# A vision tower with a mixture of experts: the high and the low half of the second FFN matrix side by side, in one 512-column product

## The chip, the cores and the metric

The kernel runs on one core of a Trainium2 chip, as one program with one launch. The metric is the device time in microseconds (us). The kernel before takes 1067.86 us, the median of three runs (1067.56 to 1068.58).

## The reference, cut to what matters

Sixteen images of 256 tokens with 256 features pass through a token mixer (16 independent sequences), a gated linear recurrence, and then an FFN with one shared and eight routed experts. Only the FFN bears on the change:

```python
def new_gelu(x):
    c = math.sqrt(2.0 / math.pi)
    return 0.5 * x * (1.0 + jnp.tanh(c * (x + 0.044715 * x * x * x)))

def _moe_forward(x, Wfc_s, bfc_s, Wproj_s, bproj_s, Wr, Wfc, bfc, Wproj, bproj):
    xf = x.reshape(Bb * Tt, C)                       # C = 256, hidden 1024
    shared = new_gelu(xf @ Wfc_s + bfc_s) @ Wproj_s + bproj_s
    ...                                              # softmax over 8 experts, top 2, gates sum to 1
    for e in range(N_EXPERTS):
        h = new_gelu(xf @ Wfc[e] + bfc[e]) @ Wproj[e] + bproj[e]
        routed = routed + h * gate[:, e:e + 1]
    return (shared + routed).reshape(Bb, Tt, C)
```

The class token's row is the same for all images before the FFN, and the kernel computes it once.

## The kernel before, in words

**Precision.** The big products run in fp32r, a format that the matrix engine takes in one pass but rounds. To keep accuracy each operand is split into a high half (rounded) and a low half (the rest), and a product is the sum of three: high x high, high x low and low x high. For the second FFN product the operands are G, the hidden activations (`GH`, `GL`, 1024 hidden rows in 8 parts of 128, by 256 tokens), and the second matrix (`W2H`, `W2L`, 8 parts of 128 rows by 256 columns). G is the stationary operand (128 x 128, loaded as weights), the matrix is the moving one.

**First stage, the mixer (`steps`).** A software pipeline over the images: step t projects image t, and at the same time computes later phases of images t-1 to t-4. The last phase is the shared expert for image t-4: for j in 0 to 7 the first product `fc` (6 products), and, three parts later (`LAG = 3`), the second one, `project_hidden` for part j-3. VectorE (`DVE`) computes `GL` for each part (`low_g`, L1077), waits for it on `y_ps` at the end, adds the bias into `yb` (L1425) and the residual (L1428). The accumulators `y_loop` share the two PSUM banks of `ps_nd` with the mixer's numerator and denominator (L843), of which they take the first half.

**Second stage, the experts (`experts_tensor`, `experts_vector`, `experts_pool`).** Tokens were scattered into lists by expert. Eight experts follow each other, each with its blocks of 256 tokens (36 in all here, read from register bounds). The matrix engine (`PE`) does per block: `fc` for the parts 0 to 7, the hidden parts 0 to 4 between them, the transposes of the next block's rows (L892), and the hidden parts 5 to 7. At the first hidden part it waits until `y_done` says that VectorE has read the accumulators. VectorE does per block: `GL` for eight parts, the low half of the next tokens (`xl`, L1485), then `rows_to` (L1543), which waits until the row adds of the block before have landed (`added`), a copy of `info` (L1480), two adds of the bias to `yt` (L1548), one for each half of the tokens, and two products with the gate to `yb` (L1552). Then the next block's `GL`. In the last block of an expert it also subtracts the low halves of the next expert's weights between the `GL` operations (`low_w`, L1518); at its end it counts `expert_done`.

GpSimd (`POOL`) waits for `y_done` of each block, starts two indirect DMAs that add the 256 rows to the output (L603), and, when an expert starts, before its blocks: `load_high` and `load_stage`, four DMAs of 1 MB for the next expert, each on the same DMA queue as the row adds. Its small `carrier` operations mark where it waited: `carrier_pool` for `added`, `carrier_y` for `y_done`.

**Semaphores.** `gh_done`, `gl_done`: a part of GH or GL is there. `y_ps`: the sum of one half of the tokens is complete. `y_done`, `yt_done`: VectorE's operations at L1425 / L1552, and at L1548. `w_split`: the low halves of an expert are there.

## Time and profile before

| | |
|---|---|
| median of three runs | 1067.86 us |
| the profiled execution, its own time | 1067.47 us |
| its span, first to last instruction | 1065.7 us |
| mean granted TensorE clock | 0.955 |
| PE busy | 91% |
| DVE busy | 66% |
| ACT busy | 43% |
| POOL busy | 35% |

The span has a beginning (about 120 us) in which the pipeline fills, the mixer in its regular steps of 32 us to about 600 us, and the experts from there to the end. Busy time of PE counts the modelled ends of its products, which overlap; what a product takes from the engine is seen from the distance of two starts in the timeline. In a timeline "x2" means that two instructions of one kind were merged to one row.

### The profile page before, as it was taken

Reading aid. Unit: us, or ns where it says so; the run is one execution under the profiler, and the core shown is the slowest. Engines: PE = TensorE matmul, PEld = TensorE weight load, DVE = VectorE, ACT = ScalarE, POOL = GpSimd, SP = SyncE. Lnnn points to the kernel's source line nnn. Section 1 sums busy time; section 2 is a strip of 40 time slices with the busy share of each in tenths; the row PEclk is TensorE's granted clock in tenths of the full one; section 3 lists DMA queues with packets and bytes.
Section 4 is the critical chain, followed back from the end, with each engine's and each line's share of the span. In section 5 each row is a group of like instructions: output and inputs, shape, how many; then the busy total and the mean of one; then the engine's idle time right before and its main releaser. Section 6 shows DMA issues by size and latency. Waiting matters only on the chain.

```text
span 1065.7 us, 21605 instructions
## 1 busy us (share of the span) xinstructions
PE 970.7 (91%) x6889; PEld 899.1 (84%) x6890; DVE 705.3 (66%) x2095; ACT 454.7 (43%) x1139; POOL 378.0 (35%) x468
## 2 busy tenths in 40 slices
PE   5787788999999999999788999999999999999995
PEld 3555587888888888888787899999999999999995
DVE  3458788887887877888776446464645546564643
ACT  2011143344444444444332255555555555555553
POOL 4232554242343243343421133443243424243222
PEclk9667799999999999999999799999999999999998
DMA  9300610111100111100011372837272633664322
GB/s 275 104 10 11 173 40 1 40 42 40 40 20 22 38 40 40 40 20 15 32 45 41 122 202 45 208 52 190 40 212 45 168 79 80 163 129 126 45 40 31
DMA packets 48164, 82.68 MB, mean 78 GB/s; under 512 B 6416, under 2 KB 30883, under 8 KB 48132
## 3 DMA queue, kind: packets, MB, share of 16 engines
q0 software_dynamic: 31056, 57.46, 22.3%
q1 hardware_dynamic: 17076, 24.84, 7.9%
q8 instruction: 15, 0.25, 0.1%
q14 instruction: 17, 0.14, 0.0%
HBM read 55.32 MB, written 26.96 MB: 77 GB/s over the span
## 4 chain that ended last, share of the span: by engine, by line
PE 41%; issue 27%; DVE 15%; POOL 13%; ACT 1%; POOLq 1%; DMA 0%; DVEq 0%; SPq 0%; ACTq 0%
PE ps_nd L657 14%; PE ps_proj L642 8%; POOL out L603 5%; PE ps_proj L722 5%; PE ps_ri L642 4%; DVE rden L1254 3%; PE ps_ip L642 3%; POOL v_rows L498 2%; PE ps_nd L843 2%; POOL h L561 1%; PE ps_h L830 1%; PE ps_h L815 1%; POOL rstd L494 1%; PE ps_t L729 1%; DVE A L1386 1%
## 5 line engine op out<-in xcount | busy, mean ns | idle before, releaser
L1077 DVE TENSOR_TENSOR GL<-g_act,GH 128x256 fp32r<-128x256 f32 (+1 forms) x424 | 185.3, 439 | 189.4 <-ACT GH L955 170.3
L657 PE MATMUL ps_nd<-w2h,GH 128*128 128x256 f32 x832 | 248.9, 299 | 24.9 <-DVE GL L1077 13.5
L950 ACT ACTIVATE g_act<-ps_proj,fcb 128x256 f32<-128x256 f32 (+1 forms) x280 | 130.8, 468 | 308.8 <-PE ps_proj L642 300.6
L657 PE MATMUL ps_nd<-w2l,GH 128*128 128x256 f32 x832 | 235.8, 283 | 0.0
L657 PE MATMUL ps_nd<-w2h,GL 128*128 128x256 f32 x832 | 234.7, 282 | 0.0
L657 PEld LDWEIGHTS ps_nd<-w2h,GH 128*128 128x128 f32 x832 | 158.4, 190 | 35.2 <-DVE GL L1077 14.0
L955 ACT CAST GH<-g_act 128x256 fp32r<-128x256 f32 x416 | 161.4, 397 | 0.0
L657 PEld LDWEIGHTS ps_nd<-w2l,GH 128*128 128x128 f32 x832 | 158.8, 191 | 0.0
L657 PEld LDWEIGHTS ps_nd<-w2h,GL 128*128 128x128 f32 x832 | 158.1, 190 | 0.0
L642 PE MATMUL ps_proj<-xh,w1h 128*128 128x256 f32 x544 | 116.3, 295 | 9.3 <-issue 4.4
L603 POOL DMA_INDIRECT out<-yb,rows_to x72 | 114.8, 1595 | 16.7 <-issue 12.8
L642 PE MATMUL ps_proj<-xl,w1h 128*128 128x256 f32 x544 | 110.3, 285 | 0.0
L642 PE MATMUL ps_proj<-xh,w1l 128*128 128x256 f32 x544 | 108.7, 281 | 0.0
L491 POOL TENSOR_TENSOR ve<-mv,eps 128x2 f32<-128x2 f32 x48 | 10.4, 218 | 276.6 <-DVE mv L1092 276.6
L642 PEld LDWEIGHTS ps_proj<-xh,w1h 128*128 128x128 f32 x544 | 85.3, 190 | 16.7 <-issue 10.8
L722 PE MATMUL ps_proj<-wproj,x 65*128 65x256 f32 x256 | 78.9, 459 | 12.8 <-DMA x<-x 6.4
L642 PEld LDWEIGHTS ps_proj<-xl,w1h 128*128 128x128 f32 x544 | 84.2, 190 | 0.0
L642 PEld LDWEIGHTS ps_proj<-xh,w1l 128*128 128x128 f32 x544 | 83.7, 189 | 0.0
L722 PEld LDWEIGHTS ps_proj<-wproj,x 65*128 65x128 f32 x256 | 66.8, 327 | 19.5 <-issue 15.0
L498 POOL DMA_INDIRECT v_rows<-v,slots x64 | 68.2, 1065 | 35.9 <-DVE slots L1362 19.1
L331 POOL TENSOR_TENSOR carrier_y<-minus_half 1x1 f32<-1x1 f32 x36 | 6.6, 183 | 175.3 <-DVE yb L1552 175.3
L961 ACT ACTIVATE E<-ps_proj 128x256 f32<-128x256 f32 x32 | 12.3, 383 | 118.2 <-PE ps_proj L722 118.1
(271 smaller groups left out, 1943.4 us busy)
## 6 DMA issues: line engine op xcount, KB each, us to landing
R<-v_rows SPq DMA_DIRECT2D x37, 260.0 KB
w1h<-fc_w POOLq DMA_DIRECT2D x9, 1024.0 KB
w2h<-pj_w POOLq DMA_DIRECT2D x9, 1024.0 KB
stage<-fc_w POOLq DMA_DIRECT2D x9, 1024.0 KB
stage<-pj_w POOLq DMA_DIRECT2D x9, 1024.0 KB
v_rows<-tail_rows SPq DMA_DIRECT2D x16, 260.0 KB, 3.0
x<-x SPq DMA_DIRECT2D x16, 256.0 KB, 3.6
out<-yb SPq DMA_DIRECT2D x16, 256.0 KB, 2.1
```

The source lines that it names most:

```text
L494: pool.tensor_tensor(rstd[i][:], ve[i][:], minus_half[:], ALU.pow).then_inc(rstd_done[i], 1)
L498: pool.indirect_dma_start(out=v_rows, out_offset=bass.IndirectOffsetOnAxis(ap=where_to, axis=0), in_=source, in_offset=None).then_inc(sema ...
L603: pool.indirect_dma_start(out=out, out_offset=bass.IndirectOffsetOnAxis(ap=rows_to[:, a:a + 1], axis=0), in_=yb[:, a, :], in_offset=None, ...
L642: last = pe.matmul(dst, w[a][:, k, cols], rhs, start=(q == 0), stop=(q == len(parts) - 1))
L657: last = pe.matmul(banks[a], g[:, j, a * P:(a + 1) * P], w[i][:, j, :], start=(j == 0 and q == 0), stop=(j == HT - 1 and q == 2))
L722: last = pe.matmul(ps_proj[:, h, :], head_view(par, lt, h), wproj[:, h, :], start=True, stop=True)
L843: last = pe.matmul(ps_nd[:, tt, :], ewT[:, s, tt * P:(tt + 1) * P], E[:, s, :], start=(s == 0), stop=(s == LT - 1))
L950: act.activation(g_act[:, j % G_SLOTS, 0:width], banks[j % len(banks)][:, 0:width], ACT.Gelu_apprx_tanh, bias=fcb[i][:, j:j + 1]).then_inc ...
L955: act.copy(GH[:, j, :], g_act[:, j % G_SLOTS, :]).then_inc(gh_done, 1)
L961: act.activation(E[:, lt, M:2 * M].rearrange("p (h d) -> p h d", h=H), ps_proj[:, :, D:2 * D], ACT.Exp).then_inc(exp_done, 1)
L1077: dve.tensor_tensor(GL[:, j, 0:width], g_act[:, j % G_SLOTS, 0:width], GH[:, j, 0:width].bitcast(F32), ALU.subtract).then_inc(gl_done, 1)
L1254: dve.reciprocal(rden[:, tt, :], ps_nd[:, tt, M:2 * M]).then_inc(recip_done, 1)
```

## The change

`W2H` and `W2L` become one buffer `W2` with 512 columns per part: the high half in columns 0 to 255, the low half in 256 to 511. The accumulators become 512 columns wide, a whole PSUM bank. Per hidden part and half of the tokens there are now two products: GH with all 512 columns (its left half is high x high, its right half high x low), and GL with the left 256 columns, added onto the left half. VectorE adds the left half and the bias, and then the right half, in two more operations per block or image. PE's wait at the first hidden part of an expert's block is now on `yt_done`.

```diff
-        W2H = [sb(f"w2h{i}", [P, HT, M], F32R) for i in range(2)]
-        W2L = [sb(f"w2l{i}", [P, HT, M], F32R) for i in range(2)]
+        W2 = [sb(f"w2_{i}", [P, HT, 2 * M], F32R) for i in range(2)]
...
-        y_loop = [ps_nd[:, 0, 0:M], ps_nd[:, 1, 0:M]]
+        y_loop = [ps_nd[:, 0, :], ps_nd[:, 1, :]]
...
-            pool.dma_start(W2H[i][:], pj_of(g)).then_inc(high_loaded, 16)
+            pool.dma_start(W2[i][:, :, 0:M], pj_of(g)).then_inc(high_loaded, 16)
...
+        def low_part(eng, i, q, parts):
+
+            half = parts // 2
+            if q < half:
+                n = FT * HID // half
+                cols = slice(q * n, (q + 1) * n)
+                return eng.tensor_tensor(flat(W1L[i])[:, cols], flat(stage1)[:, cols],
+                                         flat(W1H[i])[:, cols].bitcast(F32), ALU.subtract)
+            n = HT // half
+            js = slice((q - half) * n, (q - half + 1) * n)
+            return eng.tensor_tensor(W2[i][:, js, M:2 * M], stage2[:, js, :],
+                                     W2[i][:, js, 0:M].bitcast(F32), ALU.subtract)
...
             for a in range(2):
-                for q, (g, w) in enumerate(((GH, W2H), (GH, W2L), (GL, W2H))):
-                    last = pe.matmul(banks[a], g[:, j, a * P:(a + 1) * P], w[i][:, j, :],
-                                     start=(j == 0 and q == 0), stop=(j == HT - 1 and q == 2))
+                tokens = slice(a * P, (a + 1) * P)
+                pe.matmul(banks[a], GH[:, j, tokens], W2[i][:, j, :], start=(j == 0), stop=False)
+                last = pe.matmul(banks[a][:, 0:M], GL[:, j, tokens], W2[i][:, j, 0:M], start=False,
+                                 stop=(j == HT - 1))
...
                         if j == LAG:
-                            pe.wait_ge(y_done, b * 2 + 2 * SBLK)
+                            pe.wait_ge(yt_done, b * 2 + 2)
...
-                        dve.tensor_tensor(yb[:, a, :], y_loop[a], pjb[0][:], ALU.add
+                        dve.tensor_tensor(yb[:, a, :], y_loop[a][:, 0:M], pjb[0][:], ALU.add
+                                          ).then_inc(y_half, 1)
+                    for a in range(2):
+                        dve.wait_ge(y_half, 2 * n + a + 1)
+                        dve.tensor_tensor(yb[:, a, :], yb[:, a, :], y_loop[a][:, M:2 * M], ALU.add
                                           ).then_inc(y_done, 1)
...
-                    dve.tensor_tensor(yt[:, a, :], y_loop[a], pjb[i][:], ALU.add
+                    dve.tensor_tensor(yt[:, a, :], y_loop[a][:, 0:M], pjb[i][:], ALU.add
+                                      ).then_inc(yt_half, 1)
+                for a in range(2):
+                    dve.wait_ge(yt_half, b * 2 + (a + 1))
+                    dve.tensor_tensor(yt[:, a, :], yt[:, a, :], y_loop[a][:, M:2 * M], ALU.add
                                       ).then_inc(yt_done, 1)
-                dve.wait_ge(yt_done, b * 2 + 2)
+                dve.wait_ge(yt_done, b * 2 + 4)
```

The class token's products (L922) are changed in the same way: 24 become 16, and its three additions on VectorE stay three.

PE in an expert's block, from `fc` of one part over a hidden part to the next `fc`. Before (`w2h1` and `w2l1` are the high and the low half in the second of two buffers):

```order
L642 MATMUL ps_proj<-xl0,w1h1 128x256 x2
L654 REGISTER_ALU
L657 MATMUL ps_nd<-w2h1,GH 128x256
L657 MATMUL ps_nd<-w2l1,GH 128x256
L657 MATMUL ps_nd<-w2h1,GL 128x256
L657 MATMUL ps_nd<-w2h1,GH 128x256
L657 MATMUL ps_nd<-w2l1,GH 128x256
L657 MATMUL ps_nd<-w2h1,GL 128x256
L642 MATMUL ps_ri<-xh0,w1h1 128x256 x2
```

The same place in the changed kernel, where `w2_1` is the second of the two joint buffers:

```order
L651 MATMUL ps_proj<-xl0,w1h1 128x256 x2
L663 REGISTER_ALU
L666 MATMUL ps_nd<-w2_1,GH 128x512
L667 MATMUL ps_nd<-w2_1,GL 128x256
L666 MATMUL ps_nd<-w2_1,GH 128x512
L667 MATMUL ps_nd<-w2_1,GL 128x256
L651 MATMUL ps_ri<-xh0,w1h1 128x256 x2
```

Nothing changes its place against `fc`; six products have become four.

VectorE at the end of an expert's block, from the wait for the row adds to the next block's first GL. Before:

```order
L1543 CAST rows_to<-info 128x2 [waits added]
L1480 COPY info<-R 128x8 [waits rows_loaded]
...
L1548 TENSOR_TENSOR yt<-ps_nd,pjb1 128x256 [waits y_ps]
L1547 REGISTER_ALU
L1548 TENSOR_TENSOR yt<-ps_nd,pjb1 128x256 [waits y_ps]
L1550 REGISTER_ALU
L1552 TENSOR_SCALAR yb<-yt,gate 128x256 [waits yt_done]
L1552 TENSOR_SCALAR yb<-yt,gate 128x256
```

In the changed kernel:

```order
L1554 CAST rows_to<-info 128x2 [waits added]
L1495 COPY info<-R 128x8 [waits rows_loaded]
...
L1559 TENSOR_TENSOR yt<-ps_nd,pjb1 128x256 [waits y_ps]
L1558 REGISTER_ALU
L1559 TENSOR_TENSOR yt<-ps_nd,pjb1 128x256 [waits y_ps]
L1562 REGISTER_ALU
L1563 TENSOR_TENSOR yt<-yt,ps_nd 128x256 [waits yt_half]
L1562 REGISTER_ALU
L1563 TENSOR_TENSOR yt<-yt,ps_nd 128x256 [waits yt_half]
L1565 REGISTER_ALU
L1567 TENSOR_SCALAR yb<-yt,gate 128x256 [waits yt_done]
L1567 TENSOR_SCALAR yb<-yt,gate 128x256
```

The two gate products, and with them `y_done` and the next block's `GL`, now stand behind four adds instead of two.

## Rows read from the trace of the kernel before

**Rows 1.** The page, part 1: busy us, share of span, instructions.

```profile
PE 970.7 (91%) x6889; PEld 899.1 (84%) x6890; DVE 705.3 (66%) x2095; ACT 454.7 (43%) x1139; POOL 378.0 (35%) x468
```

**Rows 2.** Windows: stretch, us; busy PE PEld DVE ACT POOL; PEclk, DMA share, GB/s.

```profile
300.00:400.00 100.00, 94.44 (x626) 84.57 (x625) 83.29 (x251) 43.94 (x103) 36.00 (x44) 1.00 0.09 32
...
800.00:900.00 100.00, 97.50 (x812) 96.30 (x811) 57.51 (x172) 53.42 (x138) 34.99 (x43) 1.00 0.42 87
```

**Rows 3.** PE timeline, one block (start, us, instruction); last row: groups, 600 to 1066.

```profile
843.74 0.60 PE L892 MATMUL ps_t<-ident,R 128*128 128x128 f32 x4
...
850.74 0.28 PE L657 MATMUL ps_nd<-w2h,GH 128*128 128x256 f32 x1
...
851.45 0.40 PE L642 MATMUL ps_proj<-xh,w1h 128*128 128x256 f32 x2
...
855.71 0.60 PE L892 MATMUL ps_t<-ident,R 128*128 128x128 f32 x4
...
L657 PE MATMUL ps_nd<-w2l,GH 128*128 128x256 f32 x576 | 162.2, 282 | 0.0
```

**Rows 4.** Timeline of PE and its weight loads (PEld) in the mixer.

```profile
384.70 0.37 PE L804 MATMUL ps_ri<-route_hl,xh 128*128 128x16 f32 x2
384.92 0.37 PE L804 MATMUL ps_ri<-route_hl,xl 128*128 128x16 f32 x2
...
389.55 1.97 PE L830 MATMUL ps_h<-outw_sb,YT 128*128 128x256 f32 x8
391.36 1.02 PE L843 MATMUL ps_nd<-E,ewT 128*128 128x512 f32 x2
...
391.79 0.19 PEld L843 LDWEIGHTS ps_nd<-E,ewT 128*128 128x128 f32 x1 [0.24 <-issue]
392.22 0.19 PEld L843 LDWEIGHTS ps_nd<-E,ewT 128*128 128x128 f32 x1 [0.24 <-issue]
```

**Rows 5.** DVE timeline, end of a common block; in brackets idle before, releaser.

```profile
845.60 0.16 DVE L1543 CAST rows_to<-info 128x2 uint32<-128x2 f32 x1
...
846.15 0.78 DVE L1548 TENSOR_TENSOR yt<-ps_nd,pjb 128x256 f32<-128x256 f32 x2
846.97 0.62 DVE L1552 TENSOR_SCALAR yb<-yt,gate 128x256 f32<-128x256 f32 x2
848.73 0.42 DVE L1077 TENSOR_TENSOR GL<-g_act,GH 128x256 fp32r<-128x256 f32 x1 [1.14 <-issue]
```

**Rows 6.** Timelines of DVE and PE at two hand-overs to the next expert.

```profile
772.59 0.50 PE L642 MATMUL ps_proj<-xh,w1h 128*128 128x256 f32 x2 [1.01 <-DVE xl L1485]
...
775.11 0.43 DVE L1077 TENSOR_TENSOR GL<-g_act,GH 128x256 fp32r<-128x256 f32 x1 [0.47 <-issue]
...
831.29 0.42 DVE L1077 TENSOR_TENSOR GL<-g_act,GH 128x256 fp32r<-128x256 f32 x1
...
831.83 0.32 PE L657 MATMUL ps_nd<-w2h,GH 128*128 128x256 f32 x1
...
834.24 0.50 PE L642 MATMUL ps_proj<-xh,w1h 128*128 128x256 f32 x2 [1.50 <-issue]
...
836.75 0.43 DVE L1077 TENSOR_TENSOR GL<-g_act,GH 128x256 fp32r<-128x256 f32 x1 [0.66 <-ACT GH L955]
```

**Rows 7.** Timelines of POOL and DVE: late row adds, second block of two experts.

```profile
795.17 0.18 POOL L331 TENSOR_TENSOR carrier_pool<-minus_half 1x1 f32<-1x1 f32 x1 [5.20 <-DMA out<-yb,rows_to]
...
858.10 0.18 POOL L331 TENSOR_TENSOR carrier_pool<-minus_half 1x1 f32<-1x1 f32 x1 [6.50 <-DMA out<-yb,rows_to]
...
858.05 0.17 DVE L1543 CAST rows_to<-info 128x2 uint32<-128x2 f32 x1 [0.40 <-DMA out<-yb,rows_to]
```

**Rows 8.** Timelines of PE and DVE, end of a mixer step.

```profile
381.53 0.39 PE L657 MATMUL ps_nd<-w2h,GH 128*128 128x256 f32 x1 [0.64 <-issue]
...
383.01 0.69 DVE L1428 TENSOR_TENSOR yb<-yb,h 128x512 f32<-128x512 f32 x1
385.50 0.42 DVE L1247 TENSOR_TENSOR E<-ps_proj,E 128x256 f32<-128x256 f32 x1 [1.80 <-ACT xr L967]
```

More of the change, by code:

```diff
@@ L274, in vit_tower @@
         y_ps, y_done, yt_done, sum_done = sem("y_ps"), sem("y_done"), sem("yt_done"), sem("sum_done")
+        y_half, yt_half = sem("y_half"), sem("yt_half")
         info_done, added = sem("info_done"), sem("added")
@@ L480, in split_low @@
             for q in range(PARTS) if part is None else (part,):
-                stage, high, low = ((stage1, W1H, W1L), (stage2, W2H, W2L))[q * 2 // PARTS]
-                n = 2 * FT * HID // PARTS
-                cols = slice((q % (PARTS // 2)) * n, (q % (PARTS // 2) + 1) * n)
-                last = pool.tensor_tensor(flat(low[i])[:, cols], flat(stage)[:, cols],
-                                          flat(high[i])[:, cols].bitcast(F32), ALU.subtract)
+                last = low_part(pool, i, q, PARTS)
             if part in (None, PARTS - 1):
@@ L920, in experts_tensor @@
             for j in range(HT):
-                for q, (g, w) in enumerate(((GH, W2H), (GH, W2L), (GL, W2H))):
-                    last = pe.matmul(y_loop[0][0:2, :], g[:, j, 0:2], w[0][:, j, :],
-                                     start=(j == 0 and q == 0), stop=(j == HT - 1 and q == 2))
+                pe.matmul(y_loop[0][0:2, :], GH[:, j, 0:2], W2[0][:, j, :], start=(j == 0),
+                          stop=False)
+                last = pe.matmul(y_loop[0][0:2, 0:M], GL[:, j, 0:2], W2[0][:, j, 0:M], start=False,
+                                 stop=(j == HT - 1))
             last.then_inc(y_ps, 2)
@@ L1496, in experts_vector @@
             dve.wait_ge(y_ps, 2 * b + 2)
-            for a in range(2):
-                cols = slice(a * P, (a + 1) * P)
-                dve.tensor_tensor(c_y[:, cols], y_loop[0][0:1, cols], pjb[0][0:1, cols], ALU.add
-                                  ).then_inc(y_done, 1)
+            dve.tensor_tensor(c_y[:], y_loop[0][0:1, 0:M], pjb[0][0:1, :], ALU.add
+                              ).then_inc(y_done, 2)
             dve.wait_ge(y_done, 2 * b + 2)
+            dve.tensor_tensor(c_y[:], c_y[:], y_loop[0][0:1, M:2 * M], ALU.add).then_inc(yt_done, 2)
+            dve.wait_ge(yt_done, 2)
             dve.tensor_tensor(c_y[:], c_y[:], c_h1[:], ALU.add).then_inc(cls_base, 1)
@@ L1510, in low_w @@
             def low_w(g, i, j):
-                stage, high, low = ((stage1, W1H, W1L), (stage2, W2H, W2L))[j * 2 // HT]
-                n = 2 * FT * HID // HT
-                cols = slice((j % (HT // 2)) * n, (j % (HT // 2) + 1) * n)
                 if j == 0:
@@ L1517, in low_w @@
                     dve_wait(dve, high_loaded, g * 32 + 32, "wh")
-                last = dve.tensor_tensor(flat(low[i])[:, cols], flat(stage)[:, cols],
-                                         flat(high[i])[:, cols].bitcast(F32), ALU.subtract)
+                last = low_part(dve, i, j, HT)
                 if j == HT - 1:
```

## The prediction

> **What bounds the kernel now.** I read the busy shares first, then the stretches, then the order of instructions on the matrix engine (PE) inside one block. PE is busy 91% of the span [rows 1]; in the stretch of the experts it is 97% busy while VectorE (DVE) is at 58%, and in the stretch of the mixer PE has 94% and DVE 83% [rows 2]. So the experts hang on PE, whose clock is granted in full there (1.00, which is 2.4 GHz). A block of 256 tokens takes 11.97 us from one set of row transposes to the next [rows 3]. This repeats, except at the seven places where one expert hands over to the next; there PE idles another 1.01 us (772.59) or 1.50 us (834.24) [rows 6]. Inside a block the products stand without gaps: six of the second FFN matrix take from 850.74 to 851.45, 0.118 us each [rows 3]. The durations of 0.28 us overlap; only the distance of two starts is a price. The product count is 576 of each of the three kinds in the expert stretch, 16 per block, so 36 blocks [rows 3], and 256 of each in the mixer (16 images). The 0.118 us is not the price of 256 columns alone. Where a product has only 16 columns, two starts are still 0.111 us apart (0.22 for two) [rows 4]: that is the weight load. A product with 256 columns is then nearly in balance between load and stream, and pays a little over both.
>
> **The change on PE.** Per hidden part and half of the tokens it removes three products of 256 columns (3 x 0.118 = 0.355 us) and adds one of 512 and one of 256. The columns streamed are the same, 768; a weight load goes. The trace has no 512-column product of this format (fp32r), so I bound it. 
>
> On this the Trainium skill has a rule, in "TensorE: Matmul & The Clock Gate", section "Back-to-back issue gap": a warm product takes its columns over 2.4 GHz plus about 2.5 ns, which would be 216 and 109 ns, and a saving of 29 ns per pair. The same section gives 131 ns as a sustained distance at 512 columns; the trace speaks against that, since even 256 columns take 118 ns here [rows 3].
>
> **What the saving meets in the experts.** Four terms go back.
> (1) In the last block of an expert DVE also splits the next weights, and PE's last hidden part waits for GL: the product at 831.83 is stretched to 0.32 behind the GL operation at 831.29 [rows 6]. Work after the seventh hidden product hangs on DVE there, and so half of the block's 0.33 is not seen: 7 x 0.165 = 1.2 us.
> (2) DVE gets two more adds per block. Two such adds stand at 0.78 us [rows 5], so they add 0.78. In a common block DVE is idle before the first GL of the next block for 1.14 us [rows 5]: hidden, 0.36 to spare. Behind the adds in DVE's queue stand the two gate products, then this GL, for which PE's first hidden product waits. Where an expert ends, the idle time before that GL is only 0.66 us in one kind of loop turn and 0.47 in the other [rows 6], so GL comes 0.12 or 0.31 later. PE waits for exactly that. At 0.25 each, 7 x 0.25 = 1.7 us.
> (3) The later adds also delay y_done, and behind it in POOL's queue stand the row adds to the output and then the loads of the next weights. The row adds of an expert's first block queue behind these 4 MB of loads and land late: at 795.17 and 858.10, with PE's restart at 772.59 and 834.24, that is 22.58 and 23.86 us after the restart, the earliest and the latest of six [rows 6, 7]. DVE wants them for rows_to in the second block: at 858.05 it had waited 0.40, so it wants them 23.41 us after the restart. After the change the shorter blocks make it want them 0.33 + 0.20 earlier and the late GL 0.25 later, at 23.13; they land 0.78 later, at 23.36 to 24.64. DVE is late by 0.2 to 1.5 us. The cover: from rows_to to the first GL there are 3.13 us now [rows 5], 3.0 after the change, of which DVE needs 2.0 (rows_to to the end of yb) plus 0.78. So 0.25 is free, a bit more where y is already there. The wait on PE is 0 to 1.25 us, and I take 0.5: 6 x 0.5 = 3.0 us.
> (4) After the last block the adds stand before the last row adds and the copy of the class rows, which end the kernel: 0.8 us.
> PE's new wait on yt_done in place of y_done costs nothing: these adds stand ahead of GL in DVE's queue, and PE waits for GL in the same place.
>
> **The mixer.** A step there is a ring: PE, then DVE, then PE. PE stands 0.64 us before the last hidden product, which waits for DVE's last GL [rows 8], so only about four of the eight hidden parts lie on the path: 8 x 0.0205 = 0.16 us per step, 12 steps, 1.9 us; the four steps that drain have more of PE in them, 0.2 each: 0.8. The two new adds stand behind the last hidden product: yb's last add ends at 383.70 and DVE then idles 1.80 us until PE and ScalarE bring the next image [rows 8]; 0.78 fits in. Sum 2.7 us. If that cover were gone it would cost 16 x 0.78 = 12 us.
>
> The weights' split writes the same number of elements in two runs of 256 instead of one of 512, the load writes the same 1 KB rows: nothing for either. The class token's 24 narrow products become 16 and its adds stay three: under 0.5 us, left out.
>
> **Sum.** 11.9 + 2.7 - 1.2 - 1.7 - 3.0 - 0.8 = 7.9 us off. The profiled execution took 1067.47 us, 0.4 below the median shown (1067.86); its span is 1065.7. From the median: 1060.0.
>
> **The rivals.**
> (A) Forecast: 1060.0, between 1057 and 1062.5 as the stalls of (2) and (3) fall. Chance 0.50.
> (B) The short product's extra belongs to each product: 512 columns cost 0.226 (0.215 plus the same 0.011). The saving is 0.011 per pair: 6.3 + 1.5 = 7.8, less 0.6, 1.7, 2.4 (blocks shorten less, so rows are wanted later) and 0.8, 2.3 off: 1065.5. For it: the fp32 passes of 256 pay 0.011 too. Against: those of 512 do not. Chance 0.19.
> (C) The whole gain. Either the 256-column product behind a long one falls to 0.111 (the load's floor), pair 0.326, 0.028 saved: 16.1 in the experts and 3.7 in the mixer, less 1.6, 1.7, 4.2 (the stalls grow as the blocks shorten) and 0.8, which is 11.5 off; or the loads do not move with y_done and the stalls of (3) stay near nothing: 14.6 - 1.2 - 0.8 - 0.5: 12.1 off. Either way about 1056. Against it: POOL's queue is strictly behind y_done at the hand-over. The Trainium skill's rule above (109 ns behind a long product) would end here. Chance 0.20.
> (D) Slower. A 512-column product costs as much as the two it replaces, 0.236, because what bounds the stream is the moving rows, not the load. Then PE gains nothing, terms (2) and (4) stay with 1.7 and 0.8, and (3) with 1.0 (rows are wanted at 23.66, only the latest are late): 3.5 on, 1071.4. For it: at 256 columns load and stream cannot be told apart in this trace. Against it: the fp32 stream of 512 shows 0.43 per pass, not 0.452. It decides from about 0.230 us per long product; below that the saving, some 0.65 us for each nanosecond per pair, outweighs the terms. Chance 0.08.
> The rest, 0.03, is for what I have not seen.
>
> **The numbers.** A measurement of this kernel tells about 0.2% from no change, 2.1 us. Faster by more than that: A, C, and a little more than half of B: 0.84. Within: the rest of B and what of D comes out small, 0.08. Slower: 0.08. The range reaches over C and most of B: 1054.5 to 1066.
>
> **What would show it.** On PE the start behind a long product should come 0.216 us after it, behind a short one 0.118; a common block should be 11.64 us long instead of 11.97. At an expert's first GL, DVE's idle time should be gone. In six experts' second block rows_to should wait for the row adds by 0.2 to 1.5 us, and PE's first hidden product of the third block should come late. The mixer's step should shrink by 0.1 to 0.2 us of 32. I am wrong if a block keeps 11.97, if the block shrinks and the second blocks show no waits, or if DVE's adds come to stand in the mixer's ring.

## The result, and the profile after

The changed kernel takes 1071.22 us (median of 8 runs, 1069.7 to 1073.42), the kernel before 1067.86 in the same comparison (1067.09 to 1069.16). The ratio is 1.003, 95% interval 1.0019 to 1.0041: 3.4 us slower, where 7.9 us off were predicted. The number lies beside rival (D), 1071.4, but its mechanism does not hold, as will be seen. Two further timings of the changed kernel gave 1.0017 and 1.0047.

The first row of the page answers to [rows 1]:

```profile
PE 966.2 (90%) x6049; PEld 853.6 (80%) x6050; DVE 739.8 (69%) x2199; ACT 455.2 (43%) x1139; POOL 375.9 (35%) x468
```

The loads of PE fell from 6890 to 6050 as planned, but its busy time by 4.5 us only, and DVE has 34.5 us more. The two stretches of [rows 2]:

```profile
300.00:400.00 100.00, 94.79 (x573) 81.73 (x572) 85.41 (x257) 42.60 (x100) 35.29 (x45) 1.00 0.09 32
800.00:900.00 100.00, 97.22 (x681) 89.81 (x681) 63.18 (x189) 53.07 (x136) 33.40 (x41) 1.00 0.41 86
```

PE is as full as before in both, and still at 1.00 of its clock. PE in the experts, against [rows 3]: the start of the last five pairs of a block's second product, the product that follows them, and the starts of two consecutive blocks:

```profile
848.67 0.39 PE L666 MATMUL ps_nd<-w,GH 128*128 128x512 f32 x1
848.89 0.28 PE L667 MATMUL ps_nd<-w,GL 128*128 128x256 f32 x1
849.01 0.39 PE L666 MATMUL ps_nd<-w,GH 128*128 128x512 f32 x1
...
850.29 0.28 PE L667 MATMUL ps_nd<-w,GL 128*128 128x256 f32 x1
850.41 0.40 PE L651 MATMUL ps_proj<-xh,w1h 128*128 128x256 f32 x2
...
884.09 0.38 PE L902 MATMUL ps_t<-ident,R 128*128 128x128 f32 x2
...
895.95 0.38 PE L902 MATMUL ps_t<-ident,R 128*128 128x128 f32 x2
```

Five pairs take 850.41 - 848.67 = 1.74 us, 0.348 each: the long product is followed after 0.22 to 0.24, the short one after 0.12. A block takes 11.87 us (the median over all common blocks; the two starts above give 11.86) where it took 11.97 [rows 3].

To see where the time goes I cut each trace at two marks: the class rows' first transposes, which end the mixer, and, in the mixer, VectorE's first addition into E for the last image (15). From that mark on no new image enters; it lies in step 15, and what follows up to the class rows I call the drain. (The regular steps of 32 us thus end at about 510 us, not at 600 as said above.) Between images 5 and 15 every kernel here takes 322.3 to 323.1 us: **the live steps gained nothing and lost nothing that shows**. Half clock is the sum of the stretches at granted clock 0.50 that lie in the drain; a stretch of 10.2 us that begins 5 to 7 us before the drain's end and runs past it is in every trace, and its part ahead of the mark is counted. All times are us, from one trace each; the ratios are from the timed runs.

| kernel | mixer | its drain | half clock in it | experts to the end | ratio to before (95%) |
|---|---|---|---|---|---|
| before | 607.21 | 126.03 | 13.7 | 458.45 | |
| before, again | 607.18 | 123.86 | 5.2 | 458.88 | 0.9995 (0.9983-1.0007) |
| changed | 611.70 | 128.30 | 9.5 | 457.85 | 1.003 (1.0019-1.0041) |
| again | 612.14 | 129.91 | 17.4 | 458.27 | 1.0017 (1.0002-1.0033) |
| again2 | 615.87 | 132.43 | 23.6 | 457.83 | 1.0047 (1.003-1.0064) |
| experts_three | 611.77 | 129.86 | 17.6 | 458.55 | 1.0036 (1.0024-1.0049) |
| drain_only | 612.79 | 128.95 | 16.8 | 458.53 | 1.0048 (1.0035-1.0061) |
| mixer_three | 610.29 | 129.44 | 20.4 | 457.40 | 1.0008 (0.999-1.0026) |
| drain_three | 606.59 | 122.52 | 6.9 | 458.04 | 1.0018 (1.0006-1.003) |
| drain_three2 | 609.70 | 125.71 | 13.5 | 457.73 | 1.0019 (1.0008-1.0029) |
| no_adds | 610.56 | 126.86 | 11.7 | 456.13 | 0.9963 (0.9947-0.9979) |
| adds_only | 614.21 | 130.26 | 11.6 | 461.16 | 1.0075 (1.0052-1.0099) |
| act_half | 610.38 | 127.05 | 11.8 | 460.03 | 1.0008 (0.9995-1.002) |
| pool_bias | 606.91 | 124.95 | 12.6 | 460.64 | 1.0019 (1.001-1.0028) |
| pool_early | 606.04 | 124.94 | 12.6 | 455.77 | 0.9969 (0.9959-0.9979) |

So in the traces of the changed kernel the mixer ends 4.5 to 8.7 us later, and the experts take 0.2 to 1.1 us less. Not all of the mixer's difference is the drain's. The mark of image 15 falls between 480.85 and 484.07 us in the fifteen traces (before 481.18 and 483.32; changed 483.40, 482.23 and 483.44), and that goes with the place of the first half-clock stretch: the earlier it starts (26.7 to 29.7 us), the earlier image 5 has its mark (157.9 to 161.7), in one and the same order in kernels with the change and without. The change has no part in that. That both mixers of before end at 607.2 is therefore chance: the second one entered its drain 2.1 us later and had one 2.2 us shorter. The drains of the changed kernel are 2.3 to 8.6 us longer than those of before, at different amounts of half clock.

### The profile page after: what moved, and what is told of

Same layout as the page of the kernel before. It is cut to its first block, busy times and chain, and to the rows that moved or that the text cites. A ratio compares the mean times of both kernels' runs of the same rounds, so it can differ in the third digit from the quotient of the medians.

```text
span 1069.5 us, 20103 instructions
## 1 busy us (share of the span) xinstructions
PE 966.2 (90%) x6049; PEld 853.6 (80%) x6050; DVE 739.8 (69%) x2199; ACT 455.2 (43%) x1139; POOL 375.9 (35%) x468
## 4 chain that ended last, share of the span: by engine, by line
PE 41%; issue 27%; DVE 15%; POOL 12%; ACT 1%; POOLq 1%; DMA 0%; DVEq 0%; another core or an unknown queue 0%; SPq 0%; ACTq 0%
PE ps_nd L666 9%; PE ps_proj L651 8%; POOL out L612 5%; PE ps_proj L732 5%; PE ps_nd L667 4%; PE ps_ri L651 4%; DVE rden L1265 3%; PE ps_ip L651 2%; PE ps_nd L853 2%; POOL v_rows L507 2%; PE ps_h L840 2%; POOL h L570 1%; PE ps_h L825 1%; PE ps_t L739 1%; POOL rstd L503 1%
## 5 line engine op out<-in xcount | busy, mean ns | idle before, releaser
L666 PE MATMUL ps_nd<-w,GH 128*128 128x512 f32 x832 | 319.3, 410 | 27.5 <-DVE GL L1088 15.1
L667 PE MATMUL ps_nd<-w,GL 128*128 128x256 f32 x832 | 234.4, 282 | 0.0
L666 PEld LDWEIGHTS ps_nd<-w,GH 128*128 128x128 f32 x832 | 157.3, 189 | 64.3 <-DVE GL L1088 19.3
L667 PEld LDWEIGHTS ps_nd<-w,GL 128*128 128x128 f32 x832 | 157.4, 189 | 0.0
L732 PEld LDWEIGHTS ps_proj<-wproj,x 65*128 65x128 f32 x256 | 66.9, 328 | 19.6 <-issue 14.8
L853 PE MATMUL ps_nd<-E,ewT 128*128 128x512 f32 x128 | 60.2, 615 | 1.6 <-DVE E L1258 1.6
L1265 DVE RECIPROCAL rden<-ps_nd 128x256 f32<-128x256 f32 x32 | 55.7, 1740 | 4.3 <-PE ps_nd L853 4.3
```

The source lines that it names most:

```text
L666: pe.matmul(banks[a], GH[:, j, tokens], W2[i][:, j, :], start=(j == 0), stop=False)
L667: last = pe.matmul(banks[a][:, 0:M], GL[:, j, tokens], W2[i][:, j, 0:M], start=False, stop=(j == HT - 1))
L732: last = pe.matmul(ps_proj[:, h, :], head_view(par, lt, h), wproj[:, h, :], start=True, stop=True)
L853: last = pe.matmul(ps_nd[:, tt, :], ewT[:, s, tt * P:(tt + 1) * P], E[:, s, :], start=(s == 0), stop=(s == LT - 1))
L1265: dve.reciprocal(rden[:, tt, :], ps_nd[:, tt, M:2 * M]).then_inc(recip_done, 1)
```

## The experiments

**The same kernels again.** `again`, `again2`: the changed kernel without an edit; `before2`: the kernel before.

> The changed kernel once more, for a second profile of it. Theory 1 (the adds on VectorE cost the mixer its time): the time is again about 1071.2 us, and the class rows' transposes that end the mixer start again 3 to 4.5 us later than in the kernel before (607.2 us). Theory 2 (the loss in the mixer is the place at which PE's half-clock stretches happened to fall in one profile): the mixer's end lies anywhere from 607 to 612, and the median is still some 1071 only if something in the experts is worse than the profile showed.

> The changed kernel once more, on the chip of the next three: 3 to 4 us above the kernel before, as in its first two timings (ratios 1.003 and 1.0017). Both theories expect the same; it is the measure for them.

> The kernel before once more, for a second profile. If the half-clock stretches fall where they like, the class rows' transposes start at another time than 607.2 us, by more than 1 us; if the mixer is steady, at 607.2 within 0.5.

Measured: 1072.07, 1071.32 and 1067.72 us. The slowdown is there in all three timings of the changed kernel, between 1.8 and 5 us by the ratios. The launches of one kernel lie 2 to 8 us apart in one timing (1067.80 to 1075.57 in `again2`); the place of the half clock in the beginning is one reason, the drain another. PE's clock drops in the drain for stretches of 3.4 us, a different number of times in each launch (here `again2`, the view by windows, columns as in [rows 2]; a stretch that ends 3 us ahead of a drop, and the drop itself):

```profile
521.00:524.40 3.40, 2.06 (x18) 1.85 (x16) 2.22 (x9) 2.25 (x6) 1.27 (x3) 1.00 0.00 0
527.40:530.80 3.40, 3.40 (x17) 3.20 (x16) 2.43 (x12) 0.84 (x2) 0.98 (x2) 0.50 0.00 0
```

Granted clock 1.00 is the level of 2.4 GHz, 0.50 that of 1.2. In the first of them PE was busy for 2.06 of 3.40 us, in the 3.40 us right before the drop for 1.53; in the drain it waits time and again for VectorE (for GL 3.9 us, for the router's mask 3.6, for h 2.4, from 512 to 606 us of this trace). A single such stretch made the step that it fell in 1.3 to 1.6 us longer (steps 16 to 18). From here on a drain is compared only beside its half clock.

**The price of a product by itself.** Ahead of the experts, groups of 16 products with nothing to wait for, of 16 to 512 columns, then with 64 stationary columns, then 512 and 256 in turn; one of them:

```
+            pe.wait_ge(w_split, 2)
...
+            for q in range(16):
+                pe.matmul(ps_proj[:, 0:2, :].rearrange('p a b -> p (a b)')[:, 0:512], GH[:, q % 8, 0:P], W1H[1][:, 0, 0:512], start=True, stop=True)
...
```

> The changed kernel with series of fp32r products put in before the experts: 16 each of 16, 128, 192, 256, 320, 384, 448 and 512 columns, with 128 stationary columns, then 256 and 512 columns with 64 stationary columns, then 512 and 256 in turn. What is open: why a 512-column product takes 0.229 us and not 0.216. If the stream itself is slower than 2.4 columns per ns (a price per column), the distance rises by the same 0.0275 us per 64 columns from 256 to 512 and the 64-column load changes nothing. If each product pays a fixed 0.012 us, the slope is 0.0267 per 64 columns and 256 lies on the same line as 512. If the load of the next weights is what stretches 256 columns, 256 with 64 stationary columns falls to 0.109 while 512 keeps 0.229.

The trace of PE, start and duration of each group (the distance of two groups' starts, over 16, is the price, except that each change of size moves the first start a little):

```profile
618.21 1.85 PE L939 MATMUL ps_proj<-w1h,GH 128*128 128x16 f32 x16
619.91 1.98 PE L941 MATMUL ps_proj<-w1h,GH 128*128 128x128 f32 x16
621.73 1.98 PE L943 MATMUL ps_proj<-w1h,GH 128*128 128x192 f32 x16
623.55 2.09 PE L945 MATMUL ps_proj<-w1h,GH 128*128 128x256 f32 x16
625.48 2.51 PE L947 MATMUL ps_proj<-w1h,GH 128*128 128x320 f32 x16
627.83 2.98 PE L949 MATMUL ps_proj<-w1h,GH 128*128 128x384 f32 x16
630.64 3.42 PE L951 MATMUL ps_proj<-w1h,GH 128*128 128x448 f32 x16
633.90 3.87 PE L953 MATMUL ps_proj<-w1h,GH 128*128 128x512 f32 x16
637.61 2.03 PE L955 MATMUL ps_proj<-w1h,GH 128*64 128x256 f32 x16
639.48 3.86 PE L957 MATMUL ps_proj<-w1h,GH 128*64 128x512 f32 x16
```

Mean distance of two starts inside a group, the first distance left out: 111 to 112 ns at 16, 128 and 192 columns, 118.9 at 256, 146.7 at 320, 176.2 at 384, 203.4 at 448, 232.4 at 512; in turn 512 and 256 take 351. From 256 to 512 that is (232.4 - 118.9)/256 = 0.443 ns per column. With 64 stationary columns a load takes 0.134 us in the trace instead of 0.188, and the distance goes from 118.9 to 116.7 at 256 and from 232.4 to 231 at 512. So up to 192 columns the price does not depend on the stream (the load's 0.111 is the floor), from 256 on it rises with the columns, and at 256 the load adds 2 ns, not the 11 that I had read into it. The clock was 1.00 throughout; it is one execution.

**Without the new adds.** VectorE's two adds of the right half are left out, in the mixer and in the experts (the high x low sum is missing from the output):

```
-                    for a in range(2):
-                        dve.wait_ge(y_half, 2 * n + a + 1)
-                        dve.tensor_tensor(yb[:, a, :], yb[:, a, :], y_loop[a][:, M:2 * M], ALU.add
-                                          ).then_inc(y_done, 1)
...
```

> The changed kernel without VectorE's adds of the right half (the high x low part of the second FFN sum is left out of the images' and experts' rows). PE's products are those of the change. Theory 1: experts 3.6 us shorter than before (36 blocks x 0.10), hand-overs and second blocks as before, mixer about 1 us shorter: 1063 to 1064 us. Theory 3 (the long products themselves slow the mixer, by leaving PE longer at half clock): mixer still 3 to 4 us longer, 1067 to 1068.

Measured 1065.06 us, where the changed kernel beside it had 1072.07: the adds cost 7.0. Without them the wide product is 0.37% (0.21 to 0.53) faster than before. The seven hand-overs, each from one set of row transposes to the next with an expert's restart between them (13.1 to 14.2 us each), sum to 93.75 us (before 94.39, changed 94.68).

**Only the adds.** Three products as before, but the four adds of the change (the second add takes the left sum once more, so the rows hold it twice):

```
-                pe.matmul(banks[a], GH[:, j, tokens], W2[i][:, j, :], start=(j == 0), stop=False)
...
+                for q, (g, cols) in enumerate(() if wide else
+                                              ((GH, slice(0, M)), (GH, slice(M, 2 * M)),
+                                               (GL, slice(0, M)))):
+                    last = pe.matmul(banks[a][:, 0:M], g[:, j, tokens], W2[i][:, j, cols],
+                                     start=(j == 0 and q == 0), stop=(j == HT - 1 and q == 2))
```

> Three 256-column products everywhere as before, but VectorE's four adds as changed (the second pair adds the whole sum again, so the rows hold it twice). Theory 1: the adds' full price without PE's gain: hand-overs 1.0, first expert 0.8, second blocks 0.6, end 0.4, mixer 3 to 4.5, together 6 to 7: 1074 to 1075 us. Theory 3: only the experts' 2.8: 1070.7 us.

Measured 1077.14, ratio 1.0075: 8 us on, where 6 to 7 were expected. The wide product, which is all that the changed kernel has besides, gives back 5 of them (1077.14 - 1072.07).

**Mixer set back, experts set back.** The same three narrow products and single adds in one stage only:

```
-                        project_hidden(pe, n, 0, j - LAG, y_loop)
+                        project_hidden(pe, n, 0, j - LAG, y_loop, wide=False)
```

> The experts as changed; the mixer with three 256-column products and one pair of adds, as before (from the joint buffer). Theories 1 and 3: the mixer ends at 607 again, the experts are 0.7 us shorter than before: 1067 us. Theory 2 (clock phase only): the mixer's end scatters and the time stays between 1067 and 1071.

> The mixer as changed (512-column products, four adds); the experts with three 256-column products and two adds, as before. Theory 1 (adds cost the mixer): mixer's end 3 to 4.5 us later than before, experts as before: 1071 to 1072 us. Theory 2 (clock phase only): 1067 to 1068.

Measured: with the mixer set back 1070.13 beside 1069.40 for before, ratio 1.0008, not told from before, where 0.7 us below it was expected; its own trace had the most half clock of the narrow drains, 20.4 us. With the experts set back 1072.16, ratio 1.0036: all of the loss stays. It is the mixer's.

**The drain alone.** `drain_three` and its repetition `drain_three2` set back only steps 16 to 19; `drain_only` is the kernel before with the change in these steps alone:

```
-                        project_hidden(pe, n, 0, j - LAG, y_loop)
+                        project_hidden(pe, n, 0, j - LAG, y_loop, wide=live(t))
...
-                    for a in range(2):
+                    for a in range(2 if live(t) else 0):
```

> The changed kernel, but in the mixer's four drain steps (16 to 19, which project no new image) the second product is again three 256-column products into the left half and VectorE adds once per row tile; live steps and experts stay as changed. Theory (the two added adds are bare on VectorE's chain of each drain step, 0.74 us in each of four): 4 x 0.74 = 3.0 us less than the changed kernel, minus 16 pairs x 4 x 0.0065 = 0.4 us that TensorE's shorter pair gave if it lay on the path there: 1068.4 to 1069.5 where the changed kernel measured 1071.2 to 1072.1, and from the first product of image 15 to the class rows' transposes some 2 to 3 us less than in a trace of the changed kernel whose clock stood alike there. Rival (the drain is paced by TensorE and by its clock, and the adds are covered as in the live steps): as the changed kernel, 1071 to 1072.

> The changed kernel with the mixer's four drain steps set back, a second time, beside the changed kernel itself. Theory (adds bare in the drain, 4 x 0.74): 2 to 4 us below again2, about level with the kernel before (ratio 0.999 to 1.001). Rival (the drain goes by TensorE and its clock): within 1 us of again2.

> The kernel before, but in the mixer's four drain steps the wide product and VectorE's four adds. Theory: 3.0 us more than before (2 to 4; ratio 1.002 to 1.004), 0.74 in each drain step's chain on VectorE, nothing in the experts. Rival: within 1 us of before.

Measured: `drain_three` 1068.32, ratio 1.0018, which alone would have left it open (the changed kernel's lowest ratio is 1.0017). On one chip with the changed kernel it is plain: `drain_three2` 1068.83 against `again2` 1071.32, 2.5 us less; and `drain_only` has the whole loss, 1072.60, 6.3 us over before by the medians and 5.1 by the ratio. The mixer of `drain_only` takes 612.79 us; the four others with a wide drain and wide live steps take 611.70 to 615.87, mean 612.87; `drain_three` and its repetition 606.59 and 609.70, between those of the six with a mixer as before (606.04 to 610.38). So the loss lies in the drain, and the rival, that the adds are covered there too, is out. The sizes do not fit as well: `drain_only` was to cost 2 to 4 us, and `drain_three2` was to stand level with before, but it and `drain_three` stand 0.19 and 0.18% above, some 2 us. Neither is explained by what follows.

The mechanism is in VectorE's order at the end of step 15 (start, us, instruction; in brackets the idle time before it). Before:

```profile
509.69 0.79 DVE L1425 TENSOR_TENSOR yb<-ps_nd,pjb 128x256 f32<-128x256 f32 x2
510.51 0.69 DVE L1428 TENSOR_TENSOR yb<-yb,h 128x512 f32<-128x512 f32 x1
511.28 0.17 DVE L1277 COPY rlg<-ps_ri 128x16 f32<-128x16 f32 x1
```

Changed:

```profile
511.90 0.78 DVE L1436 TENSOR_TENSOR yb<-ps_nd,pjb 128x256 f32<-128x256 f32 x2
512.60 0.74 DVE L1440 TENSOR_TENSOR yb<-yb,ps_nd 128x256 f32<-128x256 f32 x2
513.37 0.69 DVE L1443 TENSOR_TENSOR yb<-yb,h 128x512 f32<-128x512 f32 x1
513.98 0.17 DVE L1288 COPY rlg<-ps_ri 128x16 f32<-128x16 f32 x1
```

In a live step E of the next image follows the residual's add, and VectorE idles 1.80 us before it [rows 8]. In the changed kernel 1.11 us of that are left, and E starts 3.27 us after the first add in this step, as before (3.31 in the step of [rows 8]):

```profile
384.46 0.77 DVE L1436 TENSOR_TENSOR yb<-ps_nd,pjb 128x256 f32<-128x256 f32 x2
385.14 0.74 DVE L1440 TENSOR_TENSOR yb<-yb,ps_nd 128x256 f32<-128x256 f32 x2
385.92 0.69 DVE L1443 TENSOR_TENSOR yb<-yb,h 128x512 f32<-128x512 f32 x1
387.73 0.42 DVE L1258 TENSOR_TENSOR E<-ps_proj,E 128x256 f32<-128x256 f32 x1 [1.11 <-ACT xr L978]
```

After step 15 there is no next image: the router's first copy stands there and starts with no idle time in brackets. From the first add to that copy there were 1.59 us and are 2.08, 0.49 more. At the ends of steps 16 to 19 the distance from the first add to VectorE's next instruction behind the residual is 1.42 before and 2.08 changed, 0.66 more each (in `drain_only` 2.08 at those four and 1.59 at step 15, in `drain_three2` 1.42 to 1.44 and 2.07). So five ends are bare, 0.49 + 4 x 0.66 = 3.1 us, and `drain_three` left the one of step 15 as changed.

The drain grows by it. From the first add of one step to that of the next, in steps without half clock: into step 16 28.0 to 28.1 us where the adds of step 15 are as before and 28.5 where they are changed; into step 17 23.2 and 23.8; into step 18 18.1 to 18.2 and 18.7 (but 18.9 in `mixer_three` and 19.6 in `adds_only`, which I can't explain); and from step 19's first add to the class rows 9.17 to 9.20 and 9.82 to 9.84 in all fifteen traces. That the adds do it and not the wide product is seen in the last of these: 9.18 in `no_adds`, which has the wide product alone, and 9.84 in `adds_only`.

At step 19 the traces differ by something else. In four of them (`before2`, `changed`, `no_adds`, `act_half`) ScalarE stands still for 2.2 to 2.5 us before a gelu, released by nothing that this trace can name:

```profile
599.24 0.47 ACT L961 ACTIVATE g_act<-ps_proj,fcb 128x256 f32<-128x256 f32 x1 [2.40 <-remote]
```

A fit over 13 traces (all of the table but `no_adds` and `adds_only`; five have the wide drain) puts the price at equal clock together: drain = 121.3 + 2.6 (wide) + 0.36 x half clock, standard errors 0.6 and 0.06. With a term for ScalarE's stop it is 119.0 + 2.0 (wide) + 0.49 x half clock + 2.4 (stop), the first of these prices to 0.2, and the scatter about the fit falls from 0.9 to 0.3 us. So the changed steps cost 2.0 to 3.1 us. The wide drains also had more half clock, 17.0 us in the mean against 12.1, by either fit another 1.7 to 2.4 us. Whether the later work of PE brings that about or the launches fell so is not shown: the ranges overlap (9.5 to 23.6 and 5.2 to 20.4).

**Two repairs of the experts.** All with the mixer as before. First the right half times the gate on ScalarE, so that VectorE has four operations per block instead of six:

```
+                    act.wait_ge(yt_done, b * 2 + (a + 3))
+                    act.activation(yr[:, a, :], y_loop[a][:, M:2 * M], ACT.Copy,
+                                   scale=gate[:, a:a + 1]).then_inc(yr_done, 1)
...
+                    dve.scalar_tensor_tensor(yb[:, a, :], yt[:, a, :], gate[:, a:a + 1],
+                                             yr[:, a, :], ALU.mult, ALU.add
+                                             ).then_inc(y_done, 1)
```

> A repair: mixer as before with three products; experts with the 512-column product, but the right half is multiplied by the gate on ScalarE (idle there), and VectorE joins both halves in the gate product it does anyway, so it has four operations per block as before. If the price in the experts is VectorE's two more operations: blocks 11.87 us, hand-overs as before, mixer as before, 1067.9 - 3.6 + about 0.5 = 1064.8 us. If ScalarE's two operations delay the first gelu of the next block, blocks stay at 11.87 but hand-overs grow: 1066 to 1067.

1069.97, ratio 1.0008, above both times expected; the hand-overs grew to 96.9. ScalarE in the hand-over where PE restarts at 776.66:

```profile
776.62 0.84 ACT L1092 ACTIVATE yr<-ps_nd,gate 128x256 f32<-128x256 f32 x2 [2.50 <-DVE yt L1568]
778.50 0.84 ACT L969 ACTIVATE g_act<-ps_proj,fcb 128x256 f32<-128x256 f32 x2 [1.04 <-PE ps_proj L652]
```

The next expert's first gelu starts 1.84 us after PE's restart; in the changed kernel it is 1.02 (PE at 776.93, gelu at 777.95). The row names PE's product as what ended the wait, but that product starts as soon after the restart as in the changed kernel; what takes the other 0.8 us, after `yr` has ended at 777.46, is not shown. I put it down to the work at the turn of an expert in ScalarE's own queue, which now stands behind `yr`.

Then GpSimd works out bias x gate ahead, and VectorE needs four operations, left x gate + that, and right x gate + the sum:

```
+                pool_wait(pool, info_done, b * 4 + 3, "pgp")
+                    pool.tensor_scalar(pg[:, a, :], pjb[i][:], gate[:, a:a + 1], None, ALU.mult
+                                       ).then_inc(pg_done, 1)
...
+                    dve.scalar_tensor_tensor(yt[:, a, :], y_loop[a][:, 0:M], gate[:, a:a + 1],
+                                             pg[:, a, :], ALU.mult, ALU.add).then_inc(yt_done, 1)
...
+                    dve.scalar_tensor_tensor(yb[:, a, :], y_loop[a][:, M:2 * M], gate[:, a:a + 1],
+                                             yt[:, a, :], ALU.mult, ALU.add).then_inc(y_done, 1)
```

> The mixer's second product and adds as in the kernel before. In the experts the wide product stays, but GpSimd works out bias x gate (two operations of 128 x 256) while the products run, and VectorE does only four operations per block: left half x gate + that, right half x gate + the sum; TensorE waits for the last of them. Theory (the experts lose by two more VectorE operations in each of seven hand-overs, in the second blocks and in the tail, and gain 0.10 us of TensorE per block): the experts' whole gain of 3.6 us is left, 1064.3 to 1065.3 against 1068.2 before and 1070.1 with the mixer alone set back; the seven hand-overs together 94.0 to 94.5 us, as before, and the tail 13.9 to 14.1. Rival (the operation with two tensors and a scalar costs on VectorE what two others cost, or GpSimd's work holds up VectorE's or its own row adds): hand-overs and tail as in the kernel changed or longer, 1067.5 to 1070.

1068.50, ratio 1.0019, hand-overs 97.07: the theory failed. VectorE in a hand-over, PE's restart, and PE's first hidden product:

```profile
772.32 0.30 DVE L1562 CAST rows_to<-info 128x2 uint32<-128x2 f32 x1
772.75 0.32 DVE L1503 COPY info<-R 128x8 f32<-128x8 f32 x1
773.55 0.06 DVE L325 MEMSET carrier_pgv<- 1x1 f32 x1 [0.48 <-POOL pg L608]
...
776.32 1.23 DVE L1100 TENSOR_TENSOR GL<-g_act,GH 128x256 fp32r<-128x256 f32 x3
```

```profile
773.18 0.50 PE L656 MATMUL ps_proj<-xh,w1h 128*128 128x256 f32 x2 [0.95 <-DVE xl L1508]
...
776.80 0.50 PE L672 MATMUL ps_nd<-w,GH 128*128 128x512 f32 x1 [0.51 <-DVE GL L1100]
```

GpSimd's two operations (0.96 us each in the mean of 72) begin when the gate is there, behind hidden part 6, and end too late; and VectorE's two small operations beside them take 0.30 and 0.32 where they take 0.16 and 0.17. The Trainium skill has this in "SBUF — State Buffer", section "SBUF: two separate sides": VectorE and GpSimd share one port pair that, for the kinds of operation named there, one of them holds for a whole operation while the other is blocked. The rows agree in part only: the copy is slower beside GpSimd, but it ends at 773.07, ahead of the end of GpSimd's operation (773.50), so it was not blocked to that end. So the gate has to come earlier:

```
-                    if j == 4:
+                    if j == 1:
...
-                    if j == 5:
+                    if j == 2:
...
-                    if j == 6:
+                    if j == 3:
```

> As pool_bias, but the three operations on info that lead to the gate stand behind hidden parts 1, 2 and 3 instead of 4, 5 and 6, so that GpSimd has bias x gate ready some 4 us sooner, before VectorE's small operations at the block's end. Theory (in pool_bias VectorE waited 0.48 us for GpSimd at each hand-over and its small copies took 0.30 instead of 0.16 beside it): each hand-over 0.35 to 0.45 us shorter than there, the seven together 94.3 to 95.2 instead of 97.1, tail 14.2, and the time 2 to 3 us below pool_bias and 1 to 2 us below the kernel before (ratio 0.997 to 0.999). Rival (the four operations with two tensors and a scalar, 0.43 us each, are the hand-over's loss themselves, or GpSimd slows the weights' split now): hand-overs 96.5 or more, the time as pool_bias.

1062.94 us (1062.56 to 1065.13) against 1066.25 before: ratio 0.9969 (0.9959 to 0.9979), faster than before and than the changed kernel beside it (1071.32). The same place:

```profile
770.06 0.16 DVE L1562 CAST rows_to<-info 128x2 uint32<-128x2 f32 x1
770.35 0.17 DVE L1503 COPY info<-R 128x8 f32<-128x8 f32 x1
770.48 0.06 DVE L325 MEMSET carrier_pgv<- 1x1 f32 x1
...
773.48 0.42 DVE L1100 TENSOR_TENSOR GL<-g_act,GH 128x256 fp32r<-128x256 f32 x1 [0.35 <-ACT GH L978]
```

GL comes 2.52 us after PE's restart (770.96), as before (775.11 - 772.59 [rows 6]). The hand-overs sum to 93.29, better than the 94.3 to 95.2 expected, and the ratio lies just under the 0.997 to 0.999 expected. No run moves the gate alone in the kernel before, so how much of the gain the earlier gate would give without the wide product is not shown.

## Why the prediction was wrong, step by step

**The price of the long product** is the first step that failed. "Half of 0.43 gives 0.215 us" took a plain fp32 pass of 512 columns and halved it; the product costs 0.228 to 0.232. The pair saves 0.0065 us, not 0.0205, a block 0.10, not 0.33, and 36 blocks 3.6 us, not 11.9. It was inside my bounds (0.215 to 0.236), and in their middle stood rival (B). The sentence in (D) against a dear stream, "the fp32 stream of 512 shows 0.43 per pass, not 0.452", took its evidence from the format that was not in question. The 0.118 at 256 columns was nearly all stream: twice it, 0.236, was the nearer row, and I had set it down as an outer bound. By the Trainium skill's "N / 2.4 + 2.5" ("TensorE: Matmul & The Clock Gate", "Back-to-back issue gap") the products would be 216 and 109 ns, an estimate; they are 232.4 and 118.9 by themselves, so for fp32r neither that rule nor the section's 131 ns holds here. The 29 ns that the prediction worked out beside this rule set the rule's two products against today's measured three.

**The mixer** is the second, and it turned the sign. The live steps were to give 1.9 us through the ring: they gave nothing that shows (322.51 us over ten steps, against 323.03 and 322.67 in the two traces of before); with the pair's real saving it would have been 10 x 8 x 0.0065 = 0.5. In the drain I booked 0.8 us of gain ("the four steps that drain have more of PE in them") and let the sentence on the 1.80 us of idle time speak for all 16 steps. The cover was the wait for the next image; where there is no next image there is none. I had the price of lost cover, 0.78 a step, written down for all steps together but did not ask of which steps it was true. Measured: 3.1 us by VectorE's own rows, 2.0 to 2.6 by the fits at equal clock.

**Term (1)**, 1.2 us lost in the split blocks, is not seen: `no_adds` shortens the seven hand-overs by 0.64 of the 0.73 that seven blocks can give.

**Term (2)**, the late GL, held in kind. PE's restart, the adds and the GL at one hand-over of the changed kernel:

```profile
776.93 0.50 PE L651 MATMUL ps_proj<-xh,w1h 128*128 128x256 f32 x2 [0.99 <-DVE xl L1500]
```

```profile
777.12 0.74 DVE L1563 TENSOR_TENSOR yt<-yt,ps_nd 128x256 f32<-128x256 f32 x2
...
779.68 0.92 DVE L1088 TENSOR_TENSOR GL<-g_act,GH 128x256 fp32r<-128x256 f32 x2
```

GL comes 2.75 us after the restart instead of 2.52, and the idle time before it is gone, as said; 0.23 where 0.31 was worked out, and 0.10 at 838.36 where 0.12 was. The two last hand-overs keep idle time before GL. In sum 94.68 - 93.75 = 0.9 us, not 1.7.

**Term (3)**, the late row adds, is there but small. VectorE, and GpSimd, in the second block after 847.88:

```profile
862.93 0.17 DVE L1554 CAST rows_to<-info 128x2 uint32<-128x2 f32 x1 [0.75 <-DMA out<-yb,rows_to]
...
865.32 0.99 DVE L1088 TENSOR_TENSOR GL<-g_act,GH 128x256 fp32r<-128x256 f32 x2
```

```profile
862.98 0.18 POOL L331 TENSOR_TENSOR carrier_pool<-minus_half 1x1 f32<-1x1 f32 x1 [6.61 <-DMA out<-yb,rows_to]
```

VectorE waits 0.75 instead of 0.40 [rows 7], and 1.3 us in 3 blocks altogether, not 0.2 to 1.5 in six. The two blocks there take 12.29 and 12.05, so PE lost 0.6 us (1.6 in `again`), not 3.0. Part of it I had not named: PE's transposes at 860.17 waited 0.26 us for the next rows themselves.

```profile
860.17 0.66 PE L902 MATMUL ps_t<-ident,R 128*128 128x128 f32 x4 [0.26 <-DMA R<-v_rows]
```

In common blocks VectorE had the room that was claimed: 0.50 us of idle time are left before GL, forecast 0.36.

```profile
850.95 0.74 DVE L1563 TENSOR_TENSOR yt<-yt,ps_nd 128x256 f32<-128x256 f32 x2
851.73 0.62 DVE L1567 TENSOR_SCALAR yb<-yt,gate 128x256 f32<-128x256 f32 x2
852.84 0.43 DVE L1088 TENSOR_TENSOR GL<-g_act,GH 128x256 fp32r<-128x256 f32 x1 [0.50 <-ACT GH L966]
```

**Term (4)**, the tail: from the last block's start to the end 14.61 against 14.09 (before, again: 13.89), 0.5 to 0.7; forecast 0.8.

**Summed anew:** experts 3.6 - 0.9 - 0.6 to 1.6 - 0.6 = 0.5 to 1.5 us off (the traces: 0.75, the mean of six wide against four narrow ones that have no other edit there), drain 2.0 to 3.1 on at equal clock. That gives 0.5 to 2.6 us slower, of 3.4 measured (2.0 to 4.4). The rest is open: the greater half clock in the drain, whose cause is not shown, is one candidate, and the same rest appears in `drain_only` and, with the drain set back, in `drain_three2`.

**The rivals.** (B) had the price nearly (0.226) and the wrong mixer. (D) had the total and a point of decision at 0.230 that the price touches; but PE did gain in the experts, and the loss was in the mixer's drain, of which it says nothing. (C) is out: a short product behind a long one costs what it did. The chances were added wrongly as well: A, C and a little more than half of B make some 0.81, not 0.84.

## What to carry to other kernels

Merging two products pays only for the part of their price that is weight load: measure or bound the price by the distance of starts at the same format, and take twice the short product as the likely price of the long one unless a row of that format says less. An idle time that covers added work belongs to the steps in which something is waited for: in a software pipeline look at the prologue and the drain by themselves. When an engine off the bottleneck gets work taken from the bottleneck, fold it into operations that it does already, and let what these need be ready before the hand-over, or it returns at every hand-over.

## What the hardware showed that I had not expected

- An fp32r product costs 0.443 ns per moving column from 256 to 512 columns at granted clock 1.00 (232.4 ns at 512), and 111 to 112 ns up to 192 columns.
- PE's clock fell to 0.50 for stretches of 3.4 us in the mixer's drain, none to five of them in a trace; one such stretch made steps 16 to 18 longer by 1.3 to 1.6 us. In the beginning, where the first half-clock stretch started between 26.7 and 29.7 us, image 5's mark moved with it from 157.9 to 161.7. Both spread the launches of one kernel.
- In four of fifteen traces ScalarE stood still for 2.2 to 2.5 us in the mixer's last step; what held it is not shown.
- VectorE's copies of 128x2 and 128x8 took 0.30 and 0.32 us instead of 0.16 and 0.17 beside GpSimd's multiplication of 128x256.
